# Sine products of the rotary embedding on GpSimd, cosine products at the end of the slot

## The chip, the cores and the metric

The kernel runs on one core of a Trainium2 chip. The metric is the device time of one execution in microseconds (us). Three runs of the kernel before gave 281.36 us as median (280.41 to 284.31).

A core has engines that each work through a queue of their own and wait for each other only by semaphores: TensorE (PE in the rows, and PEld for its loading of weights), VectorE (DVE), ScalarE (ACT), GpSimd (POOL) and SyncE (SP), which issues DMA transfers here. SBUF is the memory of 128 partitions that all of them read; PSUM holds what TensorE writes.

## The reference

A transformer block on 8 sequences of 256 tokens, width 128: attention with 16 heads of size 64 and a residual with layer norm, then eight small experts of which two are weighed per token, and again a residual with layer norm. The part that the change touches is the rotary embedding of queries and keys:

```
q = input_embeds @ Wq.T + bq          # k and v likewise
q = q * cos + rotate_half(q) * sin    # k likewise
scores = einsum('bhqd,bhkd->bhqk', q, k) * scale
attn = softmax(scores, axis=-1)
out = einsum('bhqk,bhkd->bhqd', attn, v)
x = layernorm(x + out @ Wo.T + bo)
```

## The kernel before

**Units and slots.** A unit is one sequence and half of its heads (8 heads), so there are 16 units. A software pipeline of 17 slots (T = 0 to 16, `run`, L261) lets several units be in work at once. In slot T each engine does its share of: the attention of unit T (scores, exponential, product with the values, normalising); the row maxima of unit T+1 from its fourth head on and of unit T+2 up to its third head; the values of unit T+2; and the projection and rotary embedding of unit T+3 (slots 0 to 12, 13 units). In each even slot from T=2 on, called a close slot here, a sequence is finished: its heads are transposed, multiplied with Wo and normalised.

**One order per engine.** Nothing plans the order; it is written out by hand in one `slot` function per engine. Each engine's list interleaves its work by eight steps i = 0 to 7.

**ScalarE in a slot** (L686): exp of head 0, two activations that read the projection from PSUM into `raw` (L652), exp of head 1, six more of them, exp of heads 2 and 3, in close slots two copies `oT_sb` (L665), exp of head 4, two copies of the values `v_sb` (L659), exp of heads 5 to 7.

**VectorE in a slot** (L986): eight row maxima (L869, 128x512 from PSUM), four reciprocals (L882) and four normalising products (L891) of the attention, the copy `mT_sb` of the transposed maxima (L876) behind the sixth maximum, and the rotary embedding in four pieces, `rope(u, 0)` to `rope(u, 3)` (L848): the product of `raw` with the cosine table into `by_cos`, that with the sine table into `by_sin` (L829, both 128x2048 in bf16), and two rotations `roped` (L837), a difference and a sum of halves of these. In close slots the layer norm `ln_one` (L897) runs in four steps at the end; its third, `ve` (L909), is read by GpSimd, which takes the power -0.5 (`rs`, L768), and the fourth, `x` (L913), waits for that.

**What waits for whom.** TensorE's projection (L338) uses two PSUM banks. One of them holds the result of the output projection in a close slot, so the second projection of the next slot waits for `x` (L332, `take`). The copy `mT_sb` waits for the transposition L373 on TensorE, which needs ScalarE's `v_sb` copies out of the same bank. SyncE sends `mT_sb` into `qk` (L289), which the scores of the next slot wait for, and sends `roped` into `qk` with eight DMAs (L296), which the row maxima of that unit wait for, from step 5 of the next slot on (L362). These two stand in one queue on SyncE. `by_cos` and `by_sin` are single buffers, `raw` and `roped` are double.

**GpSimd** has little to do: four memsets at the start, the bias in slot 0, one `rs` in each close slot, the splitting of weights into bf16 parts in slot 13, and five `rs` at the end.

Of the kernel before, what the change touches and what calls it, by code (L numbers as in the profile page):

```python
# [6 lines left out]
ALU = mybir.AluOpType  # L7
# [6 lines left out]
P = 128  # L14
S = 256
# [41 lines left out]
def postln_block(nc, packed_b, packed_f, expert_of, out):  # L57
# [15 lines left out]
    with ExitStack() as ctx:  # L73
        def sb(name, shape, dt):
            return ctx.enter_context(nc.sbuf_tensor(name, shape, dt))

        def sem(name):
            return ctx.enter_context(nc.semaphore(name))
# [5 lines left out]
        def part_b(name):  # L84
            return in_b[:, PACK_B[name][0]:PACK_B[name][1]]
# [13 lines left out]
        sin_sb = part_b("sin")  # L99
# [9 lines left out]
        raw = sb("raw", [P, 2, 2, 2, 2, S], BF16)  # L109
        by_cos = sb("by_cos", [P, 2, 2, 2, S], BF16)  # L110
        by_sin = sb("by_sin", [P, 2, 2, 2, S], BF16)
# [78 lines left out]
        bias_step = sem("bias_step")  # L190
# [4 lines left out]
        raw_ready = sem("raw_ready")  # L195
        sin_ready = sem("sin_ready")
        cos_ready = sem("cos_ready")
        rope_ready = sem("rope_ready")
# [62 lines left out]
        def run(eng, slot):  # L261

            for T in range(UNITS + 1):
                slot(T, 0)
# [5 lines left out]
        def has(T):  # L270

            return dict(attend=0 <= T < UNITS, maxima=0 <= T + 1 < UNITS, value=0 <= T + 2 < UNITS,
                        project=0 <= T + 3 < UNITS, close=T in range(2, UNITS, 2))
# [475 lines left out]
        @block.gpsimd  # L749
        def _(pool):  # L750
            splits = [0]

            def step(ins):
                splits[0] += 1
                ins.then_inc(split_step, 1)
                pool.wait_ge(split_step, splits[0])

            def split(whole, rest, parts):

                step(nc.gpsimd.tensor_copy(parts(0), whole))  # L760
                step(nc.gpsimd.tensor_tensor(rest, whole, parts(0), ALU.subtract))
                step(nc.gpsimd.tensor_copy(parts(1), rest))
                step(nc.gpsimd.tensor_tensor(rest, rest, parts(1), ALU.subtract))
                step(nc.gpsimd.tensor_copy(parts(2), rest))

            def inverse_deviation(b):
                pool.wait_ge(ln_step, LN_STEPS * b + 3)
                nc.gpsimd.tensor_tensor(rs1[:], ve1[:], mhalf[:, 0:QT], ALU.pow).then_inc(rs1_ready, 1)  # L768

            def split_bias():  # L770

                pool.wait_ge(bias_read, 1)
                nc.gpsimd.tensor_copy(bias_p[:], bias[:]).then_inc(bias_step, 1)
                pool.wait_ge(bias_step, 1)
                nc.gpsimd.tensor_tensor(bias_r[64:P], bias[64:P], bias_p[64:P], ALU.subtract).then_inc(bias_step, 1)
                pool.wait_ge(bias_step, 2)
                nc.gpsimd.tensor_copy(bias_p[64:P], bias_r[64:P]).then_inc(bias_step, 1)
                pool.wait_ge(bias_step, 3)
                nc.gpsimd.tensor_tensor(bias_r[96:P], bias_r[96:P], bias_p[96:P], ALU.subtract).then_inc(bias_step, 1)
                pool.wait_ge(bias_step, 4)  # L780
                nc.gpsimd.tensor_copy(bias_p[96:P], bias_r[96:P]).then_inc(bias_step, 1)

            def slot(T, it):
                s = has(T)
                if s["close"]:
                    inverse_deviation((T - 2) // 2)
                if T == 0:
                    split_bias()
                if T == 13:
                    pool.wait_ge(in_late, 2 * 16)  # L790
                    split(g_sb[:], g_r[:], lambda i: g_p[:, i, :])
                    split(w1_sb[:], w1_r[:], lambda i: w1_p[:, i, :])
                    split(b2_sb[:], b2_r[:], lambda i: b2_p[:, i, :])


            for i in range(2, 4):
                q_pad, k_pad = [qk[M_ROW:P, i, a].rearrange("p g j s -> p (g j s)").bitcast(U32) for a in range(2)]
                nc.gpsimd.memset(q_pad, 0).then_inc(pool_pad, 1)
                nc.gpsimd.memset(k_pad, TWO_ONES).then_inc(pool_pad, 1)
            run(pool, slot)  # L800
            inverse_deviation(LAST)
            for p, (first, count) in enumerate(PIECES):
                pool.wait_ge(z_step, Z_STEPS * (p + 1))
                nc.gpsimd.tensor_tensor(rs2[:, 0:count], ve2[:, 0:count], mhalf[:, 0:count], ALU.pow).then_inc(rs2_ready, 1)
# [3 lines left out]
        def _(dve):  # L808
# [39 lines left out]
            def rope(u, k):  # L848

                both = slice(0, 2)  # L850
                if k == 0:
                    dve.wait_ge(rope_ready, 2 * u)
                    products(u, both, by_cos, cos_sb, cos_ready)
                if k == 1:
                    products(u, both, by_sin, sin_sb, sin_ready)
                if k == 2:
                    dve.wait_ge(cos_ready, u + 2)
                    dve.wait_ge(sin_ready, u + 2)
                    if u >= 2:
                        dve.wait_ge(qk_in[(u - 2) % 4], 16 * ROPE_DMAS * ((u - 2) // 4 + 1))  # L860
                    rotate(u, both, 0).then_inc(rope_ready, 1)
                if k == 3:
                    rotate(u, both, 1).then_inc(rope_ready, 1)
# [123 lines left out]
            def slot(T, it):  # L987
                s = has(T)
                b = (T - 2) // 2

                def find_maxima(i):
                    for u, h in maxima_at(T, i):
                        row_maxima(u, h, it)

                find_maxima(0)
                if T == 15:
                    route(0, 10)
                    route(0, 11)
                if T >= 1:
                    normalise(T - 1, 2, it)  # L1000

                find_maxima(1)
                if T == 15:
                    route(0, 12)
                    route(0, 13)
                    route(0, 14)
                if T >= 1:
                    invert_sums(T - 1, 3, it)
                if T == 15:
                    route(0, 15)  # L1010
                if T == 14:
                    route(0, 1)
                    route(0, 2)

                find_maxima(2)
                if T == 15:
                    route(0, 16)
                if T >= 1:
                    normalise(T - 1, 3, it)
                if T == 13:  # L1020
                    read_x1T(0)

                find_maxima(3)
                if T == 15:
                    read_weights(0)
                if T == 14:
                    route(0, 3)
                if s["project"]:
                    rope(T + 3, 0)
                if T == 14:  # L1030
                    route(0, 4)
                if s["attend"]:
                    invert_sums(T, 0, it)

                find_maxima(4)
                if T == 13:
                    read_x1T(1)
                if s["attend"]:
                    normalise(T, 0, it)
                if T == 15:  # L1040
                    read_weights(1)
                if s["project"]:
                    rope(T + 3, 1)

                find_maxima(5)
                if T == 14:
                    route(0, 5)
                    route(0, 6)
                if s["maxima"]:
                    read_mT(T + 1, it)  # L1050
                if s["attend"]:
                    invert_sums(T, 1, it)
                if s["project"]:
                    rope(T + 3, 2)

                find_maxima(6)
                if s["project"]:
                    rope(T + 3, 3)
                if s["attend"]:
                    normalise(T, 1, it)  # L1060
                if T == 14:
                    route(0, 7)
                if s["close"]:
                    ln_one(b, 1)

                find_maxima(7)
                if s["close"]:
                    ln_one(b, 2)
                if T == 14:
                    route(0, 8)  # L1070
                if s["close"]:
                    ln_one(b, 3)
                if s["attend"]:
                    invert_sums(T, 2, it)
                if T == 14:
                    route(0, 9)
                if s["close"]:
                    ln_one(b, 4)
# [155 lines left out]
```

## Time and profile before

| | us |
|---|---|
| median of 3 runs | 281.36 |
| the profiled execution, its own time | 279.94 |
| its span in the trace | 278.1 |
| PE busy | 229.7 (83%) |
| DVE busy | 219.3 (79%) |
| ACT busy | 168.9 (61%) |
| POOL busy | 22.3 (8%) |

The span is what the trace covers; 1.8 us of the execution's own time lie outside it. Busy shares are means over the whole span, and the slots have different limits, so the rows below are read slot by slot. The chain of work that ended last is PE for 36% and DVE for 34% of the span.

### The profile page before, as it was taken

The numbers are of one execution on the slowest core, as the hardware profiler recorded it, in microseconds if no ns is written. First come the engines' busy times: TensorE is split into PE (matmuls) and PEld (weight loads), VectorE is DVE, ScalarE is ACT, GpSimd is POOL, SyncE is SP. The second block draws the span as 40 slices with busy tenths as digits, with TensorE's granted clock in tenths as the row PEclk, the third lists the DMA queues.
The fourth block names the chain that finished last, engine by engine and source line by source line (L and its number), as shares of the span: only waits on it lengthen the run. The fifth ranks groups of instructions, "written<-read, shape, count | busy, mean of one in ns | idle before, by whom it ended". The sixth has DMA issues, their size and how long they took to land.

```text
span 278.1 us, 5219 instructions
## 1 busy us (share of the span) xinstructions
PE 229.7 (83%) x1849; PEld 133.4 (48%) x1849; DVE 219.3 (79%) x567; ACT 168.9 (61%) x329; POOL 22.3 (8%) x41
## 2 busy tenths in 40 slices
PE   1796799989888877978998698778889867999991
PEld 0232345445544534554565355445537634666671
DVE  6746878787899989789788978999866864538974
ACT  2655444958588695868677686877544638354200
POOL 5000002000100010010000001000640000100122
PEclk9999999966999998699579979999955868999998
DMA  7030343211212031111203030211300000000012
GB/s 255 4 72 1 75 86 112 48 41 38 50 28 70 13 74 32 47 45 34 67 12 78 3 77 22 57 47 32 75 4 0 3 0 4 0 2 1 38 40 75
DMA packets 12253, 12.24 MB, mean 44 GB/s; under 512 B 2732, under 2 KB 11332, under 8 KB 12228
## 3 DMA queue, kind: packets, MB, share of 16 engines
q1 hardware_dynamic: 12084, 11.65, 16.0%
q8 instruction: 15, 0.25, 0.4%
q10 hardware_dynamic: 144, 0.26, 0.3%
q14 instruction: 10, 0.08, 0.1%
HBM read 2.40 MB, written 1.05 MB: 12 GB/s over the span
## 4 chain that ended last, share of the span: by engine, by line
PE 36%; DVE 34%; ACT 9%; issue 6%; POOL 2%; DMA 1%; POOLq 0%; DVEq 0%; ACTq 0%
DVE row_max L869 11%; PE ps_t L382 7%; PE ps_s L365 6%; PE ps_o L504 5%; DVE roped L837 4%; DVE o_sb L891 4%; DVE by_sin L829 3%; PE ps_s L478 3%; PE ps_m L338 3%; PE ps_o L397 3%; ACT probs L670 3%; DVE by_cos L829 3%; PE ps_m L407 2%; ACT oT_sb L665 2%; ACT raw L652 2%
## 5 line engine op out<-in xcount | busy, mean ns | idle before, releaser
L670 ACT ACTIVATE probs<-ps_t 128x512 bf16<-128x512 f32 x128 | 76.2, 609 | 56.3 <-PE ps_t L382 56.1
L869 DVE TENSOR_REDUCE row_max<-ps_s 128x2 bf16<-128x512 f32 x128 | 86.5, 678 | 20.1 <-PE ps_s L365 10.8
L382 PE MATMUL ps_t<-qk 128*128 128x256 bf16 x256 | 58.6, 317 | 4.2 <-ACT probs L670 2.6
L652 ACT ACTIVATE raw<-ps_m,bqk 128x256 bf16<-128x256 f32 x128 | 51.0, 478 | 15.5 <-PE ps_m L338 11.7
L365 PE MATMUL ps_s<-qk 64*128 64x256 bf16 x224 | 49.6, 307 | 8.8 <-DVE row_max L869 4.5
L397 PE MATMUL ps_o<-v_sb,probs 128*128 128x65 bf16 x512 | 41.6, 210 | 2.4 <-DVE o_sb L891 2.2
L397 PEld LDWEIGHTS ps_o<-v_sb,probs 128*128 128x128 bf16 x512 | 35.8, 110 | 10.2 <-issue 3.5
L338 PE MATMUL ps_m<-in_b 128*128 128x256 bf16 x128 | 30.1, 347 | 11.2 <-DMA in_b<-in_packed_b 4.3
L382 PEld LDWEIGHTS ps_t<-qk 128*128 128x128 bf16 x256 | 15.9, 102 | 35.5 <-issue 19.1
L891 DVE TENSOR_TENSOR o_sb<-ps_o,r_sum 128x256 bf16<-128x256 f32 x64 | 26.4, 412 | 0.2
L365 PEld LDWEIGHTS ps_s<-qk 64*128 64x128 bf16 x224 | 12.9, 97 | 22.3 <-DVE row_max L869 10.3
L338 PEld LDWEIGHTS ps_m<-in_b 128*128 128x128 bf16 x128 | 13.0, 118 | 22.1 <-ACT raw L652 7.6
L837 DVE TENSOR_TENSOR roped<-by_cos,by_sin 128x1024 bf16<-128x1024 bf16 (+1 forms) x34 | 21.5, 642 | 0.7 <-issue 0.3
L741 ACT ACTIVATE hg<-ps_s,in_f 128x512 f32<-128x512 f32 x16 | 11.0, 690 | 17.4 <-PE ps_s L478 17.3
L829 DVE TENSOR_TENSOR by_cos<-raw,in_b 128x2048 bf16<-128x2048 bf16 (+1 forms) x17 | 19.6, 1154 | 1.8 <-ACT raw L652 1.7
L768 POOL TENSOR_TENSOR rs<-ve,mhalf 128x2 f32<-128x2 f32 x8 | 5.7, 711 | 178.2 <-DVE ve L909 178.2
L829 DVE TENSOR_TENSOR by_sin<-raw,in_b 128x2048 bf16<-128x2048 bf16 (+1 forms) x17 | 19.6, 1151 | 0.0
L882 DVE RECIPROCAL r_sum<-ps_o 128x4 f32<-128x4 f32 x64 | 11.0, 172 | 10.3 <-PE ps_o L397 9.7
L659 ACT CAST v_sb<-ps_m 128x512 bf16<-128x512 f32 x32 | 17.5, 611 | 2.4 <-PE ps_m L345 2.4
L355 PE MATMUL ps_s<-roped 32*128 32x256 bf16 x64 | 15.1, 407 | 4.4 <-DVE roped L837 2.4
L1100 DVE TENSOR_TENSOR hs<-hg,ps_t 128x512 f32<-128x512 f32 x16 | 11.0, 685 | 9.7 <-ACT hg L741 8.2
L665 ACT COPY oT_sb<-ps_m 128x1024 bf16<-128x1024 bf16 x16 | 15.7, 1036 | 1.0 <-PE ps_m L407 1.0
(110 smaller groups left out, 228.4 us busy)
## 6 DMA issues: line engine op xcount, KB each, us to landing
qk<-roped SPq DMA_DIRECT2D x128, 64.0 KB, 2.0
in_b<-in_packed_b SPq DMA_DIRECT2D x1, 770.0 KB, 5.8
out<-y_sb SPq DMA_DIRECT2D x3, 256.0 KB, 2.2
in_f<-in_packed_f SPq DMA_DIRECT2D x1, 586.0 KB
in_b<-in_packed_b SPq DMA_DIRECT2D x1, 512.0 KB, 4.4
in_b<-in_packed_b ACTq DMA_DIRECT2D x1, 256.0 KB, 3.7
qk<-mT_sb SPq DMA_DIRECT2D x16, 4.0 KB, 1.7
out<-y_sb SPq DMA_DIRECT2D x2, 128.0 KB, 1.9
```

Of the source, the lines that this page charges most:

```text
L338: mm = nc.tensor.matmul(ps_m[1 - a][:, half * S:half * S + S], wqk[u % 2][g][:, a, half, :], xT_sb[:, tok:tok + S], start=True, stop=True)
L365: mm = nc.tensor.matmul(ps_s[h % 2][:, t * S:t * S + S], qk[0:DH, u % 4, 0, h % 4, h // 4, t * P:t * P + P], qk[0:DH, u % 4, 1, h % 4, h / ...
L382: mm = nc.tensor.matmul(ps_t[h % 2][:, c * S:c * S + S], qk[:, u % 4, 1, h % 4, h // 4, c * P:c * P + P], qk[:, u % 4, 0, h % 4, h // 4, : ...
L397: mm = nc.tensor.matmul(ps_o[(h // 2) % 2][:, col:col + DH + 1], probs[:, h % 4, c, t * P:t * P + P], v_sb[:, (u // 2) % 2, c, head, :], s ...
L652: last = nc.scalar.activation(raw[:, u % 2, g, a, half, :], ps_m[1 - a][:, half * S:half * S + S], ACT.Identity, bias=bqk[:, a, chunk:chun ...
L659: nc.scalar.copy(v_sb[:, (u // 2) % 2, u % 2, UH * c:UH * c + UH, 0:DH], ps_m[c][:].rearrange("p (h d) -> p h d", d=DH)).then_inc(v_ready, 1)
L665: nc.scalar.copy(oT_sb[:, t].rearrange("p c s -> p (c s)"), ps_m[t][:].bitcast(BF16)).then_inc(oT_ready, 1)
L670: nc.scalar.activation(probs[:, h % 4].rearrange("p c s -> p (c s)"), ps_t[h % 2][:], ACT.Exp, scale=DH ** -0.5).then_inc(exp_done, 1)
L829: nc.vector.tensor_tensor(by_rows, raw[:, u % 2, gs].rearrange("p g a h s -> p (g a h) s"), table[:].unsqueeze(1).broadcast_to([P, 4 * (gs ...
L837: return nc.vector.tensor_tensor(r, c, s, (ALU.subtract, ALU.add)[half])
L869: nc.vector.tensor_reduce(row_max[:, u % 2, h % 4, h // 4, :], ps_s[h % 2][:].rearrange("p (t s) -> p t s", s=S), AX_X, ALU.max, negate=Tr ...
L891: nc.vector.tensor_tensor(o_sb[:, b % 2, :, head:head + 2, :].rearrange("p t h d -> p h t d"), o[:, :, 0:DH].rearrange("p (h t) d -> p h t ...
```

## The change

From unit 3 on (slot 0) the sine products are taken off VectorE and put on GpSimd, as two instructions of 128x1024 at the head of GpSimd's slot; they wait for the unit's `raw` to be complete and for the rotations of the unit before. The other three pieces of the rotary embedding stay on VectorE, but stand later: the cosine product and the first rotation on the two sides of the seventh maximum, the second rotation behind the eighth. A wait was added at the end of `split_bias`. In the diff the first `slot` is GpSimd's, and all from `route(0, 3)` on is VectorE's.

```
+            def products_sin(u):
+                pool.wait_ge(raw_ready, 4 * u + 4)
+                pool.wait_ge(rope_ready, 2 * u)
+                for g in range(2):
+                    last = nc.gpsimd.tensor_tensor(by_sin[:, g].rearrange("p a h s -> p (a h) s"),
+                                                   raw[:, u % 2, g].rearrange("p a h s -> p (a h) s"),
+                                                   sin_sb[:].unsqueeze(1).broadcast_to([P, 4, S]), ALU.mult)
+                last.then_inc(sin_ready, 1)
...
                 nc.gpsimd.tensor_copy(bias_p[96:P], bias_r[96:P]).then_inc(bias_step, 1)
+                pool.wait_ge(bias_step, 5)
...
             def slot(T, it):
                 s = has(T)
+                if s["project"]:
+                    products_sin(T + 3)
                 if s["close"]:
                     inverse_deviation((T - 2) // 2)
...
                 if T == 14:
                     route(0, 3)
-                if s["project"]:
-                    rope(T + 3, 0)
...
-                if s["project"]:
-                    rope(T + 3, 1)
-
                 find_maxima(5)
...
                 if s["attend"]:
                     invert_sums(T, 1, it)
                 if s["project"]:
-                    rope(T + 3, 2)
+                    rope(T + 3, 0)
 
                 find_maxima(6)
                 if s["project"]:
-                    rope(T + 3, 3)
+                    rope(T + 3, 2)
                 if s["attend"]:
                     normalise(T, 1, it)
...
                 find_maxima(7)
+                if s["project"]:
+                    rope(T + 3, 3)
                 if s["close"]:
                     ln_one(b, 2)
```

VectorE before, in close slot 2, from the fourth row maximum to the layer norm's `x`:

```order
L869 TENSOR_REDUCE row_max<-ps_s 128x2
L829 TENSOR_TENSOR by_cos<-raw,in_b 128x2048
L882 RECIPROCAL r_sum<-ps_o 128x4
L869 TENSOR_REDUCE row_max<-ps_s 128x2
L891 TENSOR_TENSOR o_sb<-ps_o,r_sum 128x2x2x64
L829 TENSOR_TENSOR by_sin<-raw,in_b 128x2048
L869 TENSOR_REDUCE row_max<-ps_s 128x2
L876 COPY mT_sb<-ps_m 16x128
L882 RECIPROCAL r_sum<-ps_o 128x4
L837 TENSOR_TENSOR roped<-by_cos,by_sin 128x2x2x256
L869 TENSOR_REDUCE row_max<-ps_s 128x2
L837 TENSOR_TENSOR roped<-by_cos,by_sin 128x2x2x256
```

The same place now, from the sixth row maximum on (line numbers of the changed file: L882 is the maximum, L889 the copy, L842 the product, L850 a rotation):

```order
L882 TENSOR_REDUCE row_max<-ps_s 128x2
L889 COPY mT_sb<-ps_m 16x128
L895 RECIPROCAL r_sum<-ps_o 128x4
L842 TENSOR_TENSOR by_cos<-raw,in_b 128x2048
L882 TENSOR_REDUCE row_max<-ps_s 128x2
L850 TENSOR_TENSOR roped<-by_cos,by_sin 128x2x2x256
L904 TENSOR_TENSOR o_sb<-ps_o,r_sum 128x2x2x64
L915 BN_STATS st<-ps_m 128x6 x2
L882 TENSOR_REDUCE row_max<-ps_s 128x2
L850 TENSOR_TENSOR roped<-by_cos,by_sin 128x2x2x256
L919 BN_AGGR mv<-st 128x2 x2
```

Ahead of the copy `mT_sb` there is no product left; behind it there are a product and two rotations instead of two rotations. GpSimd's queue from slot 0 to slot 4 now is (L771 the sine products, L783 to L791 the bias, L778 `rs`):

```order
L771 TENSOR_TENSOR by_sin<-raw,in_b 128x1024 x2
L783 CAST bias_p<-bias 128x128
L785 TENSOR_TENSOR bias_r<-bias,bias_p 64x128
L787 CAST bias_p<-bias_r 64x128
L789 TENSOR_TENSOR bias_r<-bias_r,bias_p 32x128
L791 CAST bias_p<-bias_r 32x128
L771 TENSOR_TENSOR by_sin<-raw,in_b 128x1024 x4
L778 TENSOR_TENSOR rs<-ve,mhalf 128x2
L771 TENSOR_TENSOR by_sin<-raw,in_b 128x1024 x4
L778 TENSOR_TENSOR rs<-ve,mhalf 128x2
```

In a close slot `rs` stands behind that slot's two products. The queues of TensorE, ScalarE and SyncE are as before.

## Rows read from the trace of the kernel before

**Rows 1.** Windows by slot T=4, 5, 6, busy us (count), granted clock, DMA.
```profile
core 0: us, PE busy (x) PEld busy (x) DVE busy (x) ACT busy (x) POOL busy (x), PEclk, DMA share, GB/s
85.53:99.04 13.51, 11.11 (x115) 6.84 (x115) 12.03 (x30) 11.26 (x23) 0.70 (x1) 1.00 0.23 55
99.04:109.25 10.21, 7.89 (x71) 4.29 (x71) 10.09 (x22) 7.12 (x16) 0.00 (x0) 0.98 0.15 37
109.25:124.29 15.04, 13.55 (x115) 8.49 (x115) 11.93 (x29) 11.43 (x23) 0.70 (x1) 0.79 0.21 49
```

**Rows 2.** ScalarE's timeline, slots 4 and 5: start, duration, instruction, [idle before].
```profile
84.92 0.60 ACT L670 ACTIVATE probs<-ps_t 128x512 bf16<-128x512 f32 x1 [0.93 <-PE ps_t L382]
...
92.18 1.17 ACT L659 CAST v_sb<-ps_m 128x512 bf16<-128x512 f32 x2
...
99.61 2.29 ACT L652 ACTIVATE raw<-ps_m,bqk 128x256 bf16<-128x256 f32 x6 [0.61 <-PE ps_m L338]
101.76 1.71 ACT L670 ACTIVATE probs<-ps_t 128x512 bf16<-128x512 f32 x3
103.36 1.07 ACT L659 CAST v_sb<-ps_m 128x512 bf16<-128x512 f32 x2
...
108.65 0.60 ACT L670 ACTIVATE probs<-ps_t 128x512 bf16<-128x512 f32 x1 [0.93 <-PE ps_t L382]
```

**Rows 3.** TensorE's timeline in slot 5: step 5's maximum and the transposition.
```profile
103.32 0.39 PE L365 MATMUL ps_s<-qk 64*128 64x256 bf16 x2
...
104.49 0.22 PE L373 MATMUL ps_m<-in_b,row_max 128*16 128x128 bf16 x1 [0.46 <-ACT v_sb L659]
```

**Rows 4.** VectorE's timeline in slots 4, 5 and 6.
```profile
93.66 0.21 DVE L876 COPY mT_sb<-ps_m 16x128 bf16<-16x128 bf16 x1 [0.21 <-PE ps_m L373]
93.89 0.18 DVE L882 RECIPROCAL r_sum<-ps_o 128x4 f32<-128x4 f32 x1
94.00 0.69 DVE L837 TENSOR_TENSOR roped<-by_cos,by_sin 128x1024 bf16<-128x1024 bf16 x1
...
99.04 0.68 DVE L869 TENSOR_REDUCE row_max<-ps_s 128x2 bf16<-128x512 f32 x1
...
104.50 1.22 DVE L829 TENSOR_TENSOR by_sin<-raw,in_b 128x2048 bf16<-128x2048 bf16 x1
105.64 0.68 DVE L869 TENSOR_REDUCE row_max<-ps_s 128x2 bf16<-128x512 f32 x1
106.23 0.20 DVE L876 COPY mT_sb<-ps_m 16x128 bf16<-16x128 bf16 x1
...
106.46 0.65 DVE L837 TENSOR_TENSOR roped<-by_cos,by_sin 128x1024 bf16<-128x1024 bf16 x1
107.03 0.67 DVE L869 TENSOR_REDUCE row_max<-ps_s 128x2 bf16<-128x512 f32 x1
...
119.06 0.20 DVE L876 COPY mT_sb<-ps_m 16x128 bf16<-16x128 bf16 x1
```

**Rows 5.** Groups by form on VectorE and GpSimd: xcount, busy us, mean ns, idle before.
```profile
L829 DVE TENSOR_TENSOR by_sin<-raw,in_b 128x2048 bf16<-128x2048 bf16 x15 | 18.2, 1213 | 0.0
...
L761 POOL TENSOR_TENSOR w_r<-in_f,w_p 128x512 f32<-128x512 f32 x1 | 1.2, 1153 | 0.1
...
L775 POOL TENSOR_TENSOR bias_r<-bias,bias_p 64x128 f32<-64x128 f32 x1 | 0.4, 423 | 0.1
```

**Rows 6.** Timelines of GpSimd and VectorE: `rs` alone, and beside a product of two SBUF inputs.
```profile
97.65 0.70 POOL L768 TENSOR_TENSOR rs<-ve,mhalf 128x2 f32<-128x2 f32 x1 [23.01 <-DVE ve L909]
...
222.07 0.80 POOL L768 TENSOR_TENSOR rs<-ve,mhalf 128x2 f32<-128x2 f32 x1 [17.05 <-DVE ve L909]
...
222.06 0.25 DVE L964 TENSOR_TENSOR sel<-in_f,top_f 128x96 f32<-128x96 f32 x1
```

**Rows 7.** SyncE's timeline and the page's DMA issues: the regrouping of `roped`.
```profile
95.92 5.09 SPq L296 DMA_DIRECT2D qk<-roped  x8
...
qk<-roped SPq DMA_DIRECT2D x128, 64.0 KB, 2.0
```

More of the change, by code:

```diff
@@ L764, in split, with products_sin @@
                 step(nc.gpsimd.tensor_copy(parts(2), rest))
+            def products_sin(u):
+                pool.wait_ge(raw_ready, 4 * u + 4)
+                pool.wait_ge(rope_ready, 2 * u)
+                for g in range(2):
+                    last = nc.gpsimd.tensor_tensor(by_sin[:, g].rearrange("p a h s -> p (a h) s"),
+                                                   raw[:, u % 2, g].rearrange("p a h s -> p (a h) s"),
+                                                   sin_sb[:].unsqueeze(1).broadcast_to([P, 4, S]), ALU.mult)
+                last.then_inc(sin_ready, 1)
             def inverse_deviation(b):
@@ L781, in split_bias @@
                 nc.gpsimd.tensor_copy(bias_p[96:P], bias_r[96:P]).then_inc(bias_step, 1)
+                pool.wait_ge(bias_step, 5)
             def slot(T, it):
                 s = has(T)
+                if s["project"]:
+                    products_sin(T + 3)
                 if s["close"]:
@@ L1027, in slot @@
                     route(0, 3)
-                if s["project"]:
-                    rope(T + 3, 0)
                 if T == 14:
@@ L1041, in slot @@
                     read_weights(1)
-                if s["project"]:
-                    rope(T + 3, 1)
                 find_maxima(5)
@@ L1053, in slot @@
                 if s["project"]:
-                    rope(T + 3, 2)
+                    rope(T + 3, 0)
                 find_maxima(6)
                 if s["project"]:
-                    rope(T + 3, 3)
+                    rope(T + 3, 2)
                 if s["attend"]:
@@ L1066, in slot @@
                 find_maxima(7)
+                if s["project"]:
+                    rope(T + 3, 3)
                 if s["close"]:
```

## The prediction

> **What bounds the kernel now.** The page gives PE 83% and DVE 79% busy and a chain that ends on both in equal parts, which names no bound. So I cut the main stretch into slots [rows 1]. The reader is to see that an odd slot (T=5) lasts 10.21 us with DVE busy for 10.09 of them, while a close slot lasts 13.51 us (T=4, clock 1.00) or 15.04 us (T=6, clock 0.79) with DVE busy for about 12.0. Two odd-even slots take about 24 to 25 us, and the change acts on both kinds.
>
> The timelines then say which half of a slot is whose. **First half of a close slot**, up to the copy mT_sb: ScalarE starts exp of head 0 at 84.92 and works without an idle row until its v_sb copies end at 92.18 + 1.17 = 93.35 [rows 2]. VectorE's mT_sb starts at 93.66, after an idle 0.21 us [rows 4]. From exp to mT_sb is 8.74 us, and it is ScalarE's. In slot 6 the same way takes 119.06 - 108.65 = 10.41 us [rows 2, 4], with TensorE at the lower clock in part of it [rows 1].
> **First half of an odd slot.** I count from 99.04, where `x` of slot 4 is done and the first maximum of slot 5 starts [rows 4]. The second projection waits for `x`, so ScalarE's six raw activations start at 99.61 and end at 101.90 (+2.86). Exps and v_sb copies follow without a gap until 104.43 (+5.39) [rows 2]. L373 starts at 104.49 and takes 0.22 [rows 3], so mT_sb could start at about 104.75 (+5.71). It starts at 106.23 (+7.19) because VectorE comes late [rows 4].
> **Second half of both**, from mT_sb to the slot's end: VectorE's list, nearly gapless. The seventh maximum starts at 107.03, the next slot's exp of head 0 at 108.65, 1.62 later [rows 2, 4].
>
> **The change part by part.** A product 128x2048 lasts 1213 ns [rows 5], but the next row starts 105.64 - 104.50 = 1.14 us after it [rows 4]; 1.14 is what VectorE's queue pays. A rotation costs 107.03 - 106.46 = 0.57.
>
> *Removed ahead of mT_sb: two products, 2.28 us.* In an odd slot VectorE now gets there at 7.19 - 2.28 = +4.91, before ScalarE and TensorE allow it, so mT_sb starts at +5.71. **Gain 1.48 us.** In a close slot nothing is gained: VectorE already waited 0.21 us there (in slot 6 at most about 0.2).
>
> *Added behind mT_sb: one product, 1.14 us.* In an odd slot cos stands ahead of the seventh maximum, in the place of the first rotation. After a wait for L373 the next but one row of VectorE comes 94.00 - 93.66 = 0.34 after mT_sb [rows 4], so cos starts at +6.05 and the seventh maximum at +7.19 instead of 107.03 - 99.04 = +7.99. The next slot's exp depends on that maximum (the mT_sb transfer leaves 1.48 earlier and is no limit): **net gain of the odd slot 0.80.** In a close slot all of the second half up to `x` is VectorE's, and `x` opens the next slot: **loss 1.14.** So a pair changes by +0.34, and six pairs (T=1 with 2, to T=11 with 12) by **+2.0 us**. Slot 0 has no `x`, and I cost it at 0. Its cover is VectorE's waits for TensorE; without that it would be 1.14 more. The sine that left the kernel's fullest engine thus buys almost nothing, since ScalarE is late next, and the cosine moved from the half with slack to the one without.
>
> *GpSimd's two products of 128x1024.* No such form in bf16 is in the trace. From 423 ns at 128 elements to 1153 at 512 [rows 5] it is 1.90 ns per element, so an estimate of 1153 + 512 x 1.90 = 2126 ns each, 4.25 us for two. From below: bf16 at half of it, 2.1 for both; from above: 1.5 times it, 6.4. I take 4.25, since the rows are the same operation on the same engine. The Trainium skill, page GPSIMD Engine Reference, section 3.1, measures 4497 ns for 2048 elements in fp32. By that the two would end 0.25 us later, and the sum be 1.5 us higher; no row here has that size.
> In an odd slot they run from +2.93 (raw done, and 0.07 from release to start, a close slot's `rs` at 97.65 follows `ve` so [rows 6]) to +7.18. The first rotation, which needs them, comes at about +7.8: no wait for the result. In a close slot raw is done near 89.1 and they end near 93.4, before mT_sb. `rs` behind them in the queue is asked for at 97.6: no wait. The added wait on bias_step costs nothing, since GpSimd has no other work then.
>
> *Both engines at SBUF.* In an odd slot cos (+6.05 to +7.19) falls inside GpSimd's second product. What that costs no row shows at this size. The nearest is `rs`, which lasts 0.70 alone and 0.80 where VectorE runs products with two SBUF inputs (0.25 us each) at the same moment [rows 6]: something is taken in turns. Bounds: 0, or the whole rest of GpSimd's instruction, 7.18 - 6.05 = 1.13 us. I take **1.13**, as the row shows one engine held up rather than both running free. It stands on the path (cos, seventh maximum, next exp), six times: **+6.8 us**.
> The Trainium skill, page SBUF — State Buffer, section "Who interferes with whom", says that a VectorE instruction with two SBUF inputs and a GpSimd instruction that reads SBUF exclude each other for the whole instruction, the first one winning. That speaks against this change in odd slots, and against any version that puts both products in the same place; the row at 222.07 agrees in kind, its 0.10 us is too short to tell whole instructions from a share.
>
> *Regrouping DMAs.* The second rotation ends later: in a close slot by 2.4 us against mT_sb and so by 1.3 against `x`. SyncE then issues eight DMAs in 5.09 us, with 2.0 to landing [rows 7]. Before, the last landed near 95.92 + 5.09 - 0.64 + 2.0 = 102.4 and step 5 of slot 5 asked at 103.32 [rows 3]. So a stall of about 0.4 appears at step 5, but L373 two rows on waits 0.46 for v_sb anyway. I cost it at 0; uncovered, 0.4 x 12 = 5 us. The next mT_sb transfer, queued behind these DMAs, still finds SyncE free.
>
> **Sum.** 2.0 + 6.8 = 8.8 us on the profiled execution's 279.94: **288.7 us**, 2.6% above the median 281.36, which lies 1.4 us over that execution. 2% either way (275.7 and 287.1) is about what can be told from no change.
>
> **Rivals.**
> A. *No turns taken at SBUF*, or bf16 products on GpSimd fast enough (both done by +6.05, so under 1.56 us each): 279.94 + 2.0 = **282**. For it: 0.10 us is little evidence, and fp32 rows speak for bf16 only by analogy. It would show as cos at 1.2 us in odd slots. Chance 0.24.
> B. *VectorE is the bound in both halves* (the other side): each of 13 sine products gives its 1.14, 14.8 us in all, **265 us**. For it: 10.09 of 10.21 us busy in the odd slot. Against: the gapless ScalarE rows up to v_sb. It decides by the idle before mT_sb: under 0.1 us, and B holds; I expect 0.8 in odd slots and 2.3 in close ones. Half of it, near 273, would come if TensorE's clock also stayed up in slots like T=6 (1.5 us between 15.04 and 13.51 each). Chance 0.12.
> C. *GpSimd slow in bf16*, 6.4 us for two: in an odd slot the turn ends at +9.3, 2.1 later; in a close one at 95.5 against cos at 94.0, 1.5. That is 6 x 3.6 = 22 more, **310 us**. Chance 0.06.
> The forecast has 0.58. Its own range is 285 (turns cost half) to 292 (step 5 uncovered, or more slots at the lower clock because TensorE idles longer before them).
>
> **Numbers.** Range 279 to 292: the forecast's and most of A. Slower by over 2%: C, and 0.42 of the forecast's 0.58, so 0.48. Within 2%: A and the rest of the forecast less a little, 0.39. Faster: B and a tail, 0.13.
>
> **What would show it.** In the odd slots: idle of about 0.8 us before mT_sb, released by L373; cos of about 2.3 us (or starting late by 1.1) while its form takes 1.2 in close slots; by_sin on GpSimd at 2.1 us each. In close slots: mT_sb where it was, counted from exp of head 0, and `x` 1.14 later. DVE's busy sum lower by 13 sines, with more idle. No idle before mT_sb would break the first step, and cos at 1.2 us everywhere the largest.

## The result, and the profile after

The changed kernel takes **294.29 us** as median of four runs (292.41 to 295.20), the kernel before 281.35 (280.41 to 284.31): a ratio of 1.0475, 95% interval 1.042 to 1.053. Slower, as forecast, but by 13 us in the medians where the sum said 8.8, and 294.3 lies above the range's end of 292. The profiled execution took 295.20 us against 279.94, its span is 293.4 against 278.1. Medians below are over all executions of a kernel, ratios and their intervals only over those within 1.5% of its fastest.

The page of the changed kernel, its busy lines (engine, us, share, count), the granted clock in 40 slices and two groups:

```profile
PE 246.1 (84%) x1849; PEld 140.1 (48%) x1849; DVE 210.9 (72%) x554; ACT 170.5 (58%) x329; POOL 77.3 (26%) x67
...
PEclk9999999999857798697788557955985599999997
...
L882 DVE TENSOR_REDUCE row_max<-ps_s 128x2 bf16<-128x512 f32 x128 | 87.5, 685 | 38.6 <-PE ps_s L365 28.1
...
L771 POOL TENSOR_TENSOR by_sin<-raw,in_b 128x1024 bf16<-128x1024 bf16 x26 | 54.6, 2120 | 110.1 <-ACT raw L652 104.9
```

VectorE is 8 us less busy, yet TensorE is 16 us more busy with the same 1849 matmuls: the same work at a lower clock. The mean granted clock, as a share of the full one, fell from 0.898 to 0.848; the clock line of the kernel before was:

```profile
PEclk9999999966999998699579979999955868999998
```

The windows by slot (T=3, 4, 5, 6, 9, 11) say where; [rows 1] has T=4, 5 and 6 of before. PEclk is the granted clock:

```profile
core 0: us, PE busy (x) PEld busy (x) DVE busy (x) ACT busy (x) POOL busy (x), PEclk, DMA share, GB/s
...
77.40:89.50 12.10, 11.96 (x71) 6.04 (x71) 9.57 (x22) 7.30 (x15) 4.20 (x2) 0.52 0.16 38
89.50:105.71 16.21, 13.37 (x120) 8.28 (x117) 11.17 (x29) 11.59 (x24) 4.90 (x3) 0.84 0.16 38
105.71:116.67 10.96, 8.43 (x74) 4.44 (x75) 9.86 (x21) 7.95 (x17) 4.19 (x2) 0.94 0.19 46
116.67:132.22 15.55, 12.84 (x114) 8.18 (x113) 11.08 (x29) 10.86 (x21) 4.90 (x3) 0.82 0.16 39
...
159.65:171.94 12.29, 12.15 (x71) 6.12 (x71) 9.59 (x22) 7.32 (x15) 4.20 (x2) 0.50 0.17 40
...
188.53:199.70 11.17, 11.04 (x71) 5.51 (x71) 9.45 (x22) 7.16 (x15) 4.19 (x2) 0.58 0.17 41
```

Before, odd slot 5 took 10.21 us with VectorE nearly gapless and TensorE at 0.98. Now slots 3 and 9, and most of slot 11, run at half the full clock, 1.2 GHz, and TensorE is the busy one (11.96 of 12.10 us in slot 3). That is a state of the odd slot that no step of the prediction contained. Slot 5 kept most of its clock (0.94), slot 7 about 0.8.

What TensorE did before the clock fell, in short windows around the wait for `x` of slot 2:

```profile
75.00:76.00 1.00, 0.71 (x4) 0.22 (x4) 0.97 (x5) 0.98 (x4) 0.00 (x0) 1.00 0.00 0
76.00:77.50 1.50, 0.00 (x0) 0.00 (x0) 0.77 (x4) 0.38 (x1) 0.70 (x1) 1.00 0.18 44
77.50:79.00 1.50, 1.46 (x10) 0.90 (x10) 1.50 (x4) 0.99 (x3) 0.00 (x0) 0.59 0.49 117
79.00:80.00 1.00, 1.00 (x7) 0.67 (x7) 0.91 (x4) 0.58 (x2) 0.00 (x0) 0.50 0.37 87
```

TensorE's own timeline has one wait of each of three kinds (start, duration, instruction, idle before and what ended it):

```profile
77.54 0.86 PE L338 MATMUL ps_m<-in_b 128*128 128x256 bf16 x4 [1.79 <-DVE x L926]
...
97.82 0.39 PE L365 MATMUL ps_s<-qk 64*128 64x256 bf16 x2 [0.94 <-DMA qk<-roped]
...
114.58 0.39 PE L365 MATMUL ps_s<-qk 64*128 64x256 bf16 x2 [1.36 <-DVE row_max L882]
```

They are the three delays that the prediction had priced one by one: `x` later, the regrouping later, the seventh maximum later behind a long cosine product. Behind each of these the clock is at 0.5 within 1.5 us. In slots 3 to 12 TensorE has eight waits of 0.9 us or more. The clock falls seven times there, each time at the end of one of the eight or within 2 us behind it; one wait, of 1.21 us, has no fall behind it. The second wait above is the end of this chain (SyncE's issues, then the last landing):

```profile
93.36 0.60 SPq L296
94.00 3.77 DMA qk<-roped
97.77 0.05 issue
97.82 0.39 PE ps_s L365 x2
```

This landing took 3.77 us where the prediction had counted 2.0, the median of [rows 7]; with 2.0 it would have come at 96.0, ahead of the time at which TensorE asked.

VectorE's cosine products and mT_sb in slots 4 and 5, and GpSimd's pair of slot 5, which answer to [rows 4] and [rows 5]:

```profile
98.92 0.21 DVE L889 COPY mT_sb<-ps_m 16x128 bf16<-16x128 bf16 x1
99.26 0.18 DVE L895 RECIPROCAL r_sum<-ps_o 128x4 f32<-128x4 f32 x1
99.36 1.21 DVE L842 TENSOR_TENSOR by_cos<-raw,in_b 128x2048 bf16<-128x2048 bf16 x1
...
111.62 0.20 DVE L889 COPY mT_sb<-ps_m 16x128 bf16<-16x128 bf16 x1
111.75 0.16 DVE L895 RECIPROCAL r_sum<-ps_o 128x4 f32<-128x4 f32 x1
111.84 2.08 DVE L842 TENSOR_TENSOR by_cos<-raw,in_b 128x2048 bf16<-128x2048 bf16 x1
```
```profile
108.65 4.19 POOL L771 TENSOR_TENSOR by_sin<-raw,in_b 128x1024 bf16<-128x1024 bf16 x2 [3.62 <-ACT raw L652]
```

GpSimd is busy until 112.84, and the cosine product that starts at 111.84 takes 0.87 us more than that of the close slot. Only slots 5 and 7 show this; in 1, 3, 9 and 11 the first half of the slot was longer, and GpSimd had finished when the cosine product started.

### The profile page after: what moved, and what is told of

It is laid out like the page before. It is cut to its first block, busy times and chain, and to the rows that moved or that the text cites. A ratio compares the mean times of both kernels' runs of the same rounds, so it can differ in the third digit from the quotient of the medians.

```text
span 293.4 us, 5245 instructions
## 1 busy us (share of the span) xinstructions
PE 246.1 (84%) x1849; PEld 140.1 (48%) x1849; DVE 210.9 (72%) x554; ACT 170.5 (58%) x329; POOL 77.3 (26%) x67
## 3 DMA queue, kind: packets, MB, share of 16 engines
q1 hardware_dynamic: 12084, 11.65, 15.1%
## 4 chain that ended last, share of the span: by engine, by line
PE 43%; DVE 13%; issue 12%; POOL 8%; SPq 5%; ACT 4%; DMA 3%; POOLq 0%; DVEq 0%; ACTq 0%
PE ps_s L365 10%; PE ps_t L382 10%; POOL by_sin L771 6%; PE ps_m L338 5%; SPq L296 5%; PE ps_o L504 4%; PE ps_o L397 4%; DVE row_max L882 3%; PE ps_s L478 3%; DMA qk<-roped 3%; DVE roped L850 2%; PE ps_m L345 2%; DVE x L926 2%; POOL rs L778 1%; PE ps_t L488 1%
## 5 line engine op out<-in xcount | busy, mean ns | idle before, releaser
L882 DVE TENSOR_REDUCE row_max<-ps_s 128x2 bf16<-128x512 f32 x128 | 87.5, 685 | 38.6 <-PE ps_s L365 28.1
L771 POOL TENSOR_TENSOR by_sin<-raw,in_b 128x1024 bf16<-128x1024 bf16 x26 | 54.6, 2120 | 110.1 <-ACT raw L652 104.9
L382 PE MATMUL ps_t<-qk 128*128 128x256 bf16 x256 | 63.4, 341 | 1.6 <-DMA qk<-mT_sb 1.1
L365 PE MATMUL ps_s<-qk 64*128 64x256 bf16 x224 | 56.2, 343 | 8.1 <-DVE row_max L882 5.6
L397 PE MATMUL ps_o<-v_sb,probs 128*128 128x65 bf16 x512 | 45.1, 220 | 2.8 <-DVE o_sb L904 2.3
L338 PE MATMUL ps_m<-in_b 128*128 128x256 bf16 x128 | 33.6, 383 | 15.0 <-DVE x L926 8.3
L397 PEld LDWEIGHTS ps_o<-v_sb,probs 128*128 128x128 bf16 x512 | 39.5, 118 | 12.7 <-issue 3.3
L338 PEld LDWEIGHTS ps_m<-in_b 128*128 128x128 bf16 x128 | 14.8, 129 | 25.8 <-DVE x L926 9.7
L778 POOL TENSOR_TENSOR rs<-ve,mhalf 128x2 f32<-128x2 f32 x8 | 5.7, 711 | 65.7 <-DVE ve L922 65.7
L842 DVE TENSOR_TENSOR by_cos<-raw,in_b 128x2048 bf16<-128x2048 bf16 (+1 forms) x17 | 21.3, 1251 | 1.7 <-ACT raw L652 1.7
L850 DVE TENSOR_TENSOR roped<-by_cos,by_sin 128x1024 bf16<-128x1024 bf16 (+1 forms) x34 | 21.8, 651 | 0.4
L345 PE MATMUL ps_m<-in_b 128*128 128x512 bf16 x32 | 14.1, 503 | 3.1 <-ACT oT_sb L665 2.3
```

The lines of the kernel that those rows point to most:

```text
L338: mm = nc.tensor.matmul(ps_m[1 - a][:, half * S:half * S + S], wqk[u % 2][g][:, a, half, :], xT_sb[:, tok:tok + S], start=True, stop=True)
L345: nc.tensor.matmul(ps_m[c][:], xT_sb[:, tok:tok + P], wv_sb[:, c * 512:c * 512 + 512], start=True, stop=True).then_inc(v_proj, 1)
L365: mm = nc.tensor.matmul(ps_s[h % 2][:, t * S:t * S + S], qk[0:DH, u % 4, 0, h % 4, h // 4, t * P:t * P + P], qk[0:DH, u % 4, 1, h % 4, h / ...
L382: mm = nc.tensor.matmul(ps_t[h % 2][:, c * S:c * S + S], qk[:, u % 4, 1, h % 4, h // 4, c * P:c * P + P], qk[:, u % 4, 0, h % 4, h // 4, : ...
L397: mm = nc.tensor.matmul(ps_o[(h // 2) % 2][:, col:col + DH + 1], probs[:, h % 4, c, t * P:t * P + P], v_sb[:, (u // 2) % 2, c, head, :], s ...
L771: last = nc.gpsimd.tensor_tensor(by_sin[:, g].rearrange("p a h s -> p (a h) s"), raw[:, u % 2, g].rearrange("p a h s -> p (a h) s"), sin_s ...
```

## The experiments

All ratios are against the kernel before, run on the same chip in the same job. Remarks behind # in the code cuts are the text's, and ... marks lines left out. The question was how much of 13 us is the new order, how much GpSimd, how much the regrouping, and whether the clock is a cause or only a companion.

**e1_move_only.** The new order without the new engine:

```
-                if s["project"]:            # GpSimd
-                    products_sin(T + 3)
...
+                if s["project"]:            # VectorE, ahead of find_maxima(5)
+                    rope(T + 3, 1)
```

> The changed order with the sine products back on VectorE, in their old place ahead of the sixth maximum. If the new places of cosine product and rotations cost the time (move theory), this is nearly as slow as the change: 289 to 295 us, with odd slots of 11 to 12 us at a lower TensorE clock. If GpSimd's work costs it (turns at SBUF, late sines), it falls back to 281 to 284 us.

Measured: 288.78 us, three executions at 288.5 to 289.2 and one at 283.81; the kernel before had 281.52 there. So with the sine products on VectorE again there is still a loss, but of 2.3 us in one execution and 7 to 7.7 in the others: how much of the 13 us the order alone costs isn't settled by this run. In the profiled one (289.06 us) TensorE waited 9.0 us in sum for `x` in five slots (4.0 in four before).

**e2_engine_only.** The reverse: the sine on GpSimd, everything else where it was.

> The sine products on GpSimd, cosine products and rotations where they were before the change. Turns theory: in odd slots the cosine product starts just behind GpSimd's first product and takes about 2 to 3 us instead of 1.2, and the first rotation waits until 7.2 us behind x, some 0.8 us later than before: 283 to 289 us. Move theory: nothing moved behind the mT_sb copy, so 277 to 283 us.

Measured: 289.97 us, ratio 1.024 (1.015 to 1.033), just above the turns theory's 283 to 289 and far from the other. VectorE's and GpSimd's timelines in slot 5:

```profile
105.60 3.02 DVE L842 TENSOR_TENSOR by_cos<-raw,in_b 128x2048 bf16<-128x2048 bf16 x1
...
110.68 0.69 DVE L850 TENSOR_TENSOR roped<-by_cos,by_sin 128x1024 bf16<-128x1024 bf16 x1 [0.25 <-issue]
```
```profile
105.42 5.17 POOL L771 TENSOR_TENSOR by_sin<-raw,in_b 128x1024 bf16<-128x1024 bf16 x2 [3.62 <-ACT raw L652]
```

This is the clearest picture of the turns. GpSimd starts first, its product of 2.10 us ends at about 107.5, and the cosine product that started at 105.60 takes 3.02 us: 1.9 of waiting and about 1.1 of work. GpSimd's pair takes 5.17 instead of 4.20, so its second product waited for the cosine product in turn. The Trainium skill, page SBUF — State Buffer, section "Who interferes with whom", gives just this: whole instructions exclude each other, and the first to start wins. The trace agrees.

**e3_after_by_group.** The changed kernel, a finer wait in TensorE's maxima (and in VectorE's rotation, which reuses `roped`):

```
-                if h == 0:
-                    need(pe, qk_in[u % 4], it * (16 * ROPE_DMAS) + 16 * ROPE_DMAS * (u // 4 + 1))
+                if h < 4:
+                    need(pe, qk_in[u % 4][h], 32 * (u // 4 + 1))
```

> The changed kernel, but the row maxima of a unit wait for the regrouping DMAs of their own group of heads only (two DMAs for each of the first four heads instead of all eight at the first). If the late regrouping at step 5 is the main loss: 3 to 6 us faster than the change, 288 to 291 us, and the 1 to 2 us waits for roped at step 5 gone. If the clock or the x path carries it: within 1.5 us of the change.

Measured: 287.02 us (283.59 to 291.38), ratio 1.018 (1.009 to 1.027), some 7 us less than the change in the median and more than either theory said. No wait for `roped` is left in its list of waits, and still its profiled execution (291.38 us) has stretches at 0.5. The regrouping weighs more than the 1.5 us of waiting for it that the trace of the changed kernel shows in slots 2 to 12.

**e4_after_tiny_sine.** The changed kernel with GpSimd's products cut to 8 elements.

> The changed kernel with GpSimd's two sine products cut to 8 elements each (the sine part of the rotation is then left out from unit 3 on). It takes away GpSimd's 4.2 us and every meeting with VectorE at SBUF, and leaves the order alone. Turns theory as predicted (6.8 us): 287 us. By the trace of the change only two cosine products took 2.1 us, so 1.8 us: 292 to 293 us.

Measured: 286.42 us, ratio 1.016 (1.008 to 1.024), again some 8 us below the change, where the visible meetings at SBUF were 1.8 us. Two different delays, each taken away alone, gave back 7.3 (e3) and 7.9 us (e4), together 15.1 of the 13 that there are, with the new order left in place in both. (e1 takes away the same meetings as e4, so it is no third delay.) Given the spreads this is a hint and no proof that they aren't independent terms. Something that they share may react to each, and the clock is the candidate.

**f1_after_fill and f4_after_fill_behind.** Idle matmuls (their result is never read) on TensorE, ahead of the wait for `x` and, as a control, behind it:

```
+            def fill(count, bank, exps):
+                pe.wait_ge(exp_done, exps)
+                for _ in range(count):
+                    nc.tensor.matmul(ps_t[bank][:, 0:P], id_sb[:], xT_sb[:, 0:P], start=True, stop=True)
...
+                if T % 2 == 1 and 3 <= T <= 11:     # f1; in f4 behind the two project() lines
+                    fill(24, 0, UH * T + 1)
                 if s["project"]:
                     project(T + 3, 0, 1, it)
                     project(T + 3, 1, 0, it)
```

> The changed kernel with 24 idle matmuls of 128 columns (about 1.3 us at the upper clock, results never read) on TensorE in odd slots 3 to 11, placed just ahead of the projection that waits for x. They fill an idle stretch and shorten nothing. Clock theory: the fall to the lower clock behind that stretch goes, odd slots 3, 9 and 11 return from 11 to 12 us to about 10.5, and the time falls by 3 to 7 us to 287 to 291. If the clock has nothing to do with that idle stretch: unchanged or slower, 294 to 297 us.

> Control for the one above: the same 24 idle matmuls in the same slots, behind the two projections instead of ahead of them, so that the wait for x stays unfilled and the matmuls lie on the path. Clock theory: the lower clock stays, and the time rises by 5 x 1 to 2 us, 298 to 304 us. If only the amount of TensorE work counts for the clock: the same as with the filling ahead, 287 to 292 us.

Measured: ahead 285.92 us (285.48 to 291.13), ratio 1.021 (1.008 to 1.035); behind 294.96, ratio 1.052 (1.040 to 1.065). Filling the wait gave back 8.4 us although it takes no work away. TensorE's timeline of f1 at the place of the 1.79 us wait:

```profile
75.48 1.50 PE L351 MATMUL ps_t<-in_b 128*128 128x128 bf16 x24
77.44 0.61 PE L338 MATMUL ps_m<-in_b 128*128 128x256 bf16 x4 [0.45 <-DVE x L933]
```

The two projections of the slot (L338) take 0.61 us there, against 0.86 at 77.54 in the changed kernel. In slots 3 to 12 of f1's trace no fall of the clock comes within 5 us of a wait for `x` any more; five of the seven that are left stand at waits of 1.1 to 1.5 us for a row maximum or for `roped`, which f1 doesn't fill. The control is less clean than I had hoped. It is not as slow as expected (298 to 304): its 24 matmuls take about 1.3 us on the path in five slots, 6.7 us, and it is no slower than the change, since its runs were granted 0.88 to 0.92 instead of 0.85 to 0.88. So idle work behind the wait raises the clock too: two of f4's waits for `x`, of 1.78 us each (ended at 160.22 and 186.94), have no fall within 9 us behind them. That the clock carries much of the loss is shown by f1 and by f2 below; that it is the wait's length alone which lets it fall is not.

**f2_after_group_fill.** The by-group wait, the filling of f1 and 16 idle matmuls at the end of odd slots.

> The changed kernel with the regrouping waits by group of heads, the 24 idle matmuls ahead of the wait for x, and 16 more at the end of odd slots, where TensorE waits behind a long cosine product. Clock theory: all three idle stretches are taken away or filled, the granted clock rises to 0.90 or more and the time to 280 to 285 us. If the move itself (1.14 us in each close slot) and the turns carry more than I read: 285 to 290 us.

Measured: 281.13 us in ten runs (280.02 to 283.10), ratio 1.0055 (1.001 to 1.010), granted clock 0.946 to 0.968. This is the change almost without its clock loss, and here its own cost can be read. The clock line of its page, VectorE around slot 5 and GpSimd beside it:

```profile
PEclk9999999999999999979999999999855699999997
```
```profile
99.05 0.73 DVE L936 TENSOR_SCALAR x<-ps_m,mv,rs 128x128 bf16<-128x128 f32 x2 [0.73 <-POOL rs L787]
99.70 0.68 DVE L892 TENSOR_REDUCE row_max<-ps_s 128x2 bf16<-128x512 f32 x1
...
105.41 0.21 DVE L899 COPY mT_sb<-ps_m 16x128 bf16<-16x128 bf16 x1 [0.32 <-PE ps_m L378]
105.64 0.18 DVE L905 RECIPROCAL r_sum<-ps_o 128x4 f32<-128x4 f32 x1
105.74 2.18 DVE L851 TENSOR_TENSOR by_cos<-raw,in_b 128x2048 bf16<-128x2048 bf16 x1
107.84 0.68 DVE L892 TENSOR_REDUCE row_max<-ps_s 128x2 bf16<-128x512 f32 x1
```
```profile
102.64 4.20 POOL L780 TENSOR_TENSOR by_sin<-raw,in_b 128x1024 bf16<-128x1024 bf16 x2 [3.63 <-ACT raw L661]
```

mT_sb starts 5.71 us behind the first maximum at 99.70, from where the prediction counted, and the cosine product takes 2.18 to 2.23 us in all six odd slots. Slots 9 and 10 from one `x` to the next (149.62 to 174.62) last 25.00 us.

**f3_before_fill.** The kernel before with filling of its own idle stretches:

```
+                if T % 2 == 1 and 3 <= T <= 11:     # ahead of the wait for x
+                    fill(16, 0, UH * T + 1)
...
+                if T % 2 == 1 and T <= 11:          # ahead of find_scores(7)
+                    fill(10, 1, UH * T + 6)
```

> The kernel before with 16 idle matmuls ahead of the wait for x in odd slots 3 to 11 and 10 ahead of the last row maximum of odd slots 1 to 11, where it idles 0.5 to 1 us before the clock falls in slots 2, 6, 8 and 10. Clock theory: fewer stretches at the lower clock (31 us before), 276 to 280 us. If its falls do not come from these idle stretches: 281 to 284 us.

Measured: **272.70 us** (271.86 to 273.27), ratio 0.974 (0.964 to 0.984), better than expected and better than both kernels without filling. Its clock and two of its slots (5, and close slot 6):

```profile
PEclk9999999999999999999999999999975979999997
```
```profile
97.95:107.90 9.95, 8.34 (x81) 4.74 (x81) 9.82 (x21) 6.86 (x15) 0.00 (x0) 1.00 0.16 37
107.90:121.70 13.80, 12.10 (x134) 7.81 (x131) 12.31 (x31) 11.55 (x24) 0.70 (x1) 1.00 0.23 54
```

Slot 6 takes 13.80 us where it took 15.04 at clock 0.79 [rows 1], and from one `x` to the next (97.30 to 121.05) 23.75 us pass.

**g1_held_tiny_sine, g2_held_no_group, g3_held_move_only, h1_held_before.** With the clock held, the parts one by one. g1 is f2 with e4's edit, g2 is f2 without e3's, g3 is f2 with e1's, and h1 is the kernel before with all additions of f2.

> The change with regrouping waits by group and TensorE's idle stretches filled, which keeps the upper clock (281.1 us), now with GpSimd's sine products cut to 8 elements each (the sine part is left out from unit 3 on). There the cosine product took 2.18 us in all six odd slots. Turns at SBUF: it takes 1.21 again, and the time falls by 6 x 0.97 = 5.8 us to about 275. If these 0.97 us lie beside other work: 279 to 281 us.

Measured: 276.14 us (274.37 to 280.63), 5.0 less than f2, ratio 0.989 (0.976 to 1.002); one `x` to the next 24.09 us (121.76 to 145.85).

> The same filled kernel (281.1 us) with the full sine products, but the row maxima wait for all eight regrouping DMAs again. If the late regrouping costs by itself at the upper clock: waits for roped of 0.5 to 1 us at step 5, 283 to 287 us. If only an idle stretch before a fall of the clock gave it weight, and L373's own wait covers it as I predicted: 281 to 282 us.

Measured: 285.93 us (282.19 to 291.70), ratio 1.016 (1.000 to 1.032), so 4.8 more than f2 and inside the range of the first theory, but with a spread as wide as that. Its list of TensorE's waits (us in total, times, longest) over slots 2 to 12:

```profile
PE ps_s L370 <- DMA qk<-roped: 5.3, 9, 1.2
```

Yet two `x` at the upper clock lie 25.01 us apart (102.24 to 127.25), as in f2, with two of these waits between them. VectorE in the odd slot of this pair, whose first maximum starts at 102.89:

```profile
109.11 0.20 DVE L898 COPY mT_sb<-ps_m 16x128 bf16<-16x128 bf16 x1
...
109.33 1.78 DVE L851 TENSOR_TENSOR by_cos<-raw,in_b 128x2048 bf16<-128x2048 bf16 x1
```

So these waits cost nothing in a slot whose clock holds, but not only because a wait for `v_sb` covers them, as predicted: mT_sb starts 0.51 us later than in f2 (+6.22 against +5.71), and the cosine product takes 0.40 less (1.78 against 2.18), because GpSimd's products end 7.14 us behind that maximum in both. The turn at SBUF covers the rest. The loss comes with the pairs of 26.0 and 26.4 us later in the same execution, which hold stretches at the lower clock, and with `x` of slot 2, 3.2 us later.

> The same filled kernel with regrouping by group and the sine products back on VectorE in their old place. Against 281.1 us it loses the turns at SBUF (5.8 us) and takes up to 6 x 0.34 us more in the first half of odd slots: 275 to 277.5 us. Against the kernel before with filling (272.7 us) it shows what the move of the cosine product costs at the upper clock, 2 to 4 us.

Measured: 276.47 us in ten runs (275.05 to 280.92), ratio 0.989 (0.983 to 0.994); one `x` to the next 24.07 us (98.02 to 122.09). That is g1's 24.09: with the clock held, the sine products on VectorE in their old place cost nothing, not the 0.34 that was expected.

> The kernel before with the very additions of the filled change: regrouping waits by group of heads, 24 idle matmuls ahead of the wait for x in odd slots 3 to 11, and 16 at the end of odd slots 1 to 11. It is the matched base for 281.1 us. If the parts add up as read (move 0.34 x 6 = 2.0 us, turns 5.8 us): 272 to 275 us. If the filling itself favours the kernel before, or its 16 matmuls delay the next slot: 276 to 279 us.

Measured: 276.60 us (275.73 to 278.23), ratio 0.986 (0.978 to 0.994), which is the second expectation: these additions suit this kernel less than f3's, and some of its pairs are longer (26.33 and 25.18 us). Which of them does it, no run parts. Where it runs steadily, one `x` to the next takes 23.73 us (173.24 to 196.97), as in f3 (23.53 to 23.89).

## Why the prediction was wrong

**The failed step is that the sum took TensorE's clock as unchanged.** The sum added 0.34 and 1.13 us per pair of slots as if the durations of everything else stayed those of the trace before. The prediction mentioned more slots at the lower clock only as the upper end of its range, and TensorE's clock as a possible gain in rival B. In fact each of the three delays makes TensorE wait longer, and the clock fell behind those waits, in odd slots too, where it had nearly held (0.92 to 1.00 in slots 3 to 11). That put 9.1 us into slots 3 to 12 which were not in the sum (worked out below). The steps one by one:

- *Removed ahead of mT_sb, +5.71.* Right. With the clock held mT_sb starts at 105.41 - 99.70 = 5.71 us behind `x`, released by the transposition, where [rows 3] had put it. Rival B is dead: VectorE waits there, and with the clock held the sine products cost nothing on VectorE (g3 against g1). The idle before mT_sb is 0.32 there and 0.28 in the close slot, not the 0.8 and 2.3 that were expected; the rest of VectorE's slack lies earlier, before row maxima and reciprocals (0.51 us ahead of the sixth maximum in f2's slot 5). At the lower clock it is another matter, in slot 3 of the change 85.12 - 77.40 = 7.72.
- *Added behind mT_sb, +0.34 a pair.* Right: 24.09 - 23.73 = 0.36 between g1 and h1 at the upper clock. Its two parts are each about 0.2 smaller than forecast, and that they cancel is luck. From `x` to mT_sb of the close slot takes 115.93 - 97.69 = 18.24 us in g1 and 192.07 - 173.24 = 18.83 in h1, a gain of 0.59 (forecast 0.80). From there to the next `x` it is 121.76 - 115.93 = 5.83 against 196.97 - 192.07 = 4.90, a loss of 0.93 (forecast 1.14).
- *GpSimd 2126 ns each.* Right: 2120 over 26 instructions, as the fp32 rows had led to expect. Rival C is dead.
- *Turns at SBUF, 1.13.* Right in kind, a little large: the cosine product grew by 2.18 - 1.21 = 0.97, and the pair by 25.00 - 24.09 = 0.91. Rival A is dead. In the changed kernel itself only two of six odd slots paid it, since the first half of the others was long enough to avoid the meeting; I had multiplied a price of the undisturbed slot by six: of the 6.8 us only about 1.8 were paid in the kernel as it is. That it still came out slower, as forecast, is in part luck, since the clock made up for the missing turns and more.
- *Regrouping at 0.* Right in a slot at the upper clock (25.01 against 25.00), though part of its cover was another than predicted (g2), and wrong in the kernel as it is: there it was one of the waits behind which the clock fell, and taking it away gave 7 us.
- *The sum.* At the upper clock the change costs 25.00 - 23.73 = 1.27 us a pair, 7.6 for six, against 8.8 predicted; the filled kernels give 281.1 against 272.7 (or 276.6 with the same filling). The rest goes with the clock. Slots 3 to 12 in five pairs, from `x` of slot 2 to `x` of slot 12 (the rows below, two of the changed kernel and two of the one before), took 214.82 - 76.75 = 138.1 us against 197.32 - 74.68 = 122.6: 15.4 more, of which 5 x 1.27 = 6.4 is that cost and 9.1 is what was not in the sum. It stands for both the lower clock and what the waits add with it; the runs do not part these two.

```profile
76.75 0.73 DVE L926 TENSOR_SCALAR x<-ps_m,mv,rs 128x128 bf16<-128x128 f32 x2 [0.73 <-POOL rs L778]
214.82 0.73 DVE L926 TENSOR_SCALAR x<-ps_m,mv,rs 128x128 bf16<-128x128 f32 x2 [0.73 <-POOL rs L778]
...
74.68 0.73 DVE L913 TENSOR_SCALAR x<-ps_m,mv,rs 128x128 bf16<-128x128 f32 x2 [0.73 <-POOL rs L768]
197.32 0.73 DVE L913 TENSOR_SCALAR x<-ps_m,mv,rs 128x128 bf16<-128x128 f32 x2 [0.73 <-POOL rs L768]
```

What stays open is the rule by which the clock falls. The waits of 0.9 to 1.8 us stand before its falls in the changed kernel, but f4 shows that work at another place of the slot counts as well, and one wait of 1.21 us ahead of a projection at 105.85 was not followed by a fall. The kernel before fits such a rule even less: its falls at about 58, 109, 133 and 160 us have no wait over 0.67 in the 3 us ahead of them, while four waits of 0.85 to 1.04 us for `x` (ended at 99.18, 124.43, 150.08 and 174.60) have no fall within 8 us behind them.

## What to carry to other kernels

When TensorE's granted clock falls and rises within a kernel, a delay of a us on another engine isn't priced by its own length: look at the granted clock slot by slot and at TensorE's idle stretches in the trace of before, and widen the range for every edit that lengthens one. Then test with idle matmuls what the clock is worth. Freeing the fullest engine helps only in the stretches where it is the last to arrive; ask for each half of a slot who waits for whom, and don't move work from the half with slack into the one without. A product on GpSimd beside a product of two SBUF inputs on VectorE took turns here by whole instructions, so place them where they can't meet, or don't split them.

## What the runs showed of the hardware

- Cheap idle matmuls in TensorE's waits made the kernel before 2.6% faster (272.7 us) with no change to its work: the granted clock of its profiled execution rose from 0.898 to 0.969.
- The time of one kernel varies along with its clock, though not in step (e1 took 289.2 us at 0.902 and 288.5 at 0.878): the four runs of the changed kernel have 0.848 to 0.878 and 292.4 to 295.2 us, e3's runs 0.869 to 0.916 and 283.6 to 291.4, while f2's ten at 0.946 to 0.968 stay within 280.0 to 283.1.
- Products of two SBUF inputs on GpSimd and VectorE exclude each other in both directions: a cosine product of 1.21 us took 3.02 when it came second, and GpSimd's pair 5.17 instead of 4.20 when its second product did.
